# Attention scores from two half-height stacks: each head of a pair in its own half of the systolic array, and the two score products of a slot moved apart

## The reference, cut to what matters

```python
q, k = rope(q), rope(k)                           # (512, 32 heads, 16)
scores = einsum('bqhd,bkhd->bhqk', q, k) / sqrt(16)
scores = scores + (1.0 - causal) * MASK_VAL
probs = softmax(scores, axis=-1)
ctx = einsum('bhqk,bkhd->bqhd', probs, v)
y = (silu(h @ W_gate.T) * (h @ W_up.T)) @ W_down.T      # beside it, on the same rows
```

## Time and profile before

| | |
|---|---|
| median of 3 runs | 745.94 us (744.32 to 747.05) |
| the profiled execution | 744.25 us |
| its span, first to last instruction | 742.1 us |
| mean granted TensorE clock | 0.964 |
| PE busy | 653.9 us, 88% |
| DVE, POOL, ACT busy | 453.2, 403.7, 280.3 us |
| score stages, both batches | 167.2 and 166.1 us |

### The profile page before, as it was taken

The page is one execution under the profiler, slowest core; times in us unless marked ns, Lnnn a source line. Parts: engine busy times, 40 slices in busy tenths (PEclk is TensorE's granted clock), DMA queues, the critical chain, the costliest instruction groups (busy, mean ns, idle before and its releaser), DMA issues. The chain is left out here.

```text
span 742.1 us, 9827 instructions
## 1 busy us (share of the span) xinstructions
PE 653.9 (88%) x3229; PEld 468.4 (63%) x3229; DVE 453.2 (61%) x1086; ACT 280.3 (38%) x501; POOL 403.7 (54%) x593
## 2 busy tenths in 40 slices
PE   1967899999989998889999998989798979797993
PEld 1756566667756776666666765678676655555571
DVE  4977778756534493887785562459454434756347
ACT  2413445444543411344444455351222534142441
POOL 6476455545343556646554534439725778344465
PEclk9989999999999999999999999999998989999997
DMA  8287575753222226967575316534200000000003
GB/s 263 80 288 227 129 203 134 212 134 77 75 72 72 57 71 198 310 151 200 140 198 144 85 36 228 190 101 160 76 1 0 1 0 1 1 0 1 0 1 113
DMA packets 59731, 82.21 MB, mean 111 GB/s; under 512 B 18057, under 2 KB 26505, under 8 KB 59681
## 3 DMA queue, kind: packets, MB, share of 16 engines
q1 hardware_dynamic: 56016, 70.31, 33.4%
q10 hardware_dynamic: 3664, 11.28, 4.1%
HBM read 63.75 MB, written 26.47 MB: 122 GB/s over the span
## 5 line engine op out<-in xcount | busy, mean ns | idle before, releaser
L731 POOL TENSOR_TENSOR w_lo<-raw,w_hi 128x512 fp32r<-128x512 f32 x98 | 129.3, 1321 | 81.7 <-ACT w_hi L1251 76.8
L1294 ACT ACTIVATE probs_T<-score_ps 128x512 f32<-128x512 f32 x160 | 95.8, 599 | 156.2 <-PE score_ps L952 132.9
L1444 DVE CUSTOM_DVE_ANT_0 score_ps<-score_ps,causal 128x128 f32<-128x128 f32 (+2 forms) x256 | 103.0, 447 | 52.9 <-PE score_ps L938 28.6
L914 PE MATMUL proj_ps<-xn_hi,w_hi 128*128 128x512 f32 x240 | 100.9, 420 | 12.2 <-DVE by_sin L1520 7.5
L752 POOL TENSOR_SCALAR_AFFINE_SELECT probs_T<-probs_T 128x256 f32<-128x256 f32 (+1 forms) x160 | 56.5, 362 | 96.6 <-ACT probs_T L1294 96.6
L915 PE MATMUL proj_ps<-xn_hi,w_lo 128*128 128x512 f32 x240 | 96.7, 403 | 0.0
L916 PE MATMUL proj_ps<-xn_lo,w_hi 128*128 128x512 f32 x240 | 96.0, 400 | 0.0
L952 PE MATMUL score_ps<-q_st,kz 100*128 100x512 f32 (+3 forms) x256 | 65.4, 316 | 8.6 <-DVE row_max L1444 8.4
L952 PEld LDWEIGHTS score_ps<-q_st,kz 100*128 100x128 f32 x256 | 47.8, 188 | 26.0 <-DVE row_max L1444 15.1
L914 PEld LDWEIGHTS proj_ps<-xn_hi,w_hi 128*128 128x128 f32 x240 | 47.1, 196 | 22.7 <-issue 12.3
L916 PEld LDWEIGHTS proj_ps<-xn_lo,w_hi 128*128 128x128 f32 x240 | 46.7, 194 | 11.4
(11 more groups left out here) (288 smaller groups left out, 1496.0 us busy)
## 6 DMA issues: line engine op xcount, KB each, us to landing
raw<-w SPq DMA_DIRECT2D x98, 256.0 KB, 2.7
rows<-rows_hi SPq DMA_DIRECT2D x32, 256.0 KB, 3.6
arranged<-tern SPq DMA_DIRECT2D x96, 85.0 KB
q_st<-rows SPq DMA_DIRECT2D x16, 384.0 KB, 4.5
kz<-rows SPq DMA_DIRECT2D x32, 192.0 KB, 4.9
rows<-rows_lo SPq DMA_DIRECT2D x16, 256.0 KB, 4.1
gate_w<-arranged ACTq DMA_DIRECT2D x4, 704.0 KB, 6.9
up_w<-arranged ACTq DMA_DIRECT2D x4, 704.0 KB, 8.3
```

Source lines behind the costliest of these rows:

```text
L731: nc.gpsimd.tensor_tensor(w_lo[n % SPLIT][:, :], raw[n % RAW][:, :], F32(w_hi[n % SPLIT][:, :]), ALU.subtract).then_inc(unit_ready, 1)
L914: nc.tensor.matmul(acc, lh, rh, start=first, stop=False)
L1294: nc.scalar.activation(probs_T[gp % 3][:, 512 * i:512 * i + 512], score_bank(b, ("b", s - LAG))[:, :], ACT.Exp, scale=0.25).then_inc(probs ...
L1444: m = nc.vector.tensor_tensor_reduce(out=block, in0=block, in1=causal[:, S - w:], scale=1.0, scalar=-3e38, op0=ALU.add, op1=ALU.max, accum ...
```

## The change

Each head gets its own 50 contraction rows: 48 as before and 2 for its maximum (high and low part), head 0 of a pair on partitions 0 to 49, head 1 on partitions 64 to 113, in q_st and in k_st, which has no zeros. A matmul of a head then uses one half of the rows of the array, and the two heads' matmuls stand next to each other in the program. A pair has 3 A tasks and 3 B tasks, each with both heads, in two banks (score_ps for A, scoreT_ps for B; neither is doubled). A slot is now: A, half of the slot's triples, B, the other half. There are 48 + 5 = 53 score slots a batch, two triples in nearly every slot, and 8 triples ahead of slot 0. The two rows that meet the maximum are written to DRAM once (`edges`) and read with the rest; clearing kz and adding −1 on VectorE fall away. There is one bank for turns instead of two in this stage. The first Q and K unit of a batch use the score_ps banks; the second Q and K unit come after two feed-forward units instead of before; all three reads of a Q or K unit are made together. The down projection's operands are split one slot earlier.

```diff
+HEAD_ROWS = ROWS + 2
-LAG = 8
-SCORE_SLOTS = 5 * PAIRS + LAG
+A_TILES = [[(3, 0)], [(2, 0), (0, 384)], [(1, 0)]]
+B_TILES = [[(0, 0)], [(1, 0), (3, 384)], [(2, 0)]]
+WIDTH = (512, 512, 256)
+TASKS = 3 * PAIRS
+LAG = 5
+SCORE_SLOTS = TASKS + LAG
-Q_UNIT, K_UNIT, V_UNIT = (0, 6, 12, 18), (1, 7, 13, 19), 2
+Q_UNIT, K_UNIT, V_UNIT = (0, 8, 12, 18), (1, 9, 13, 19), 2
 def triple_slot(k):
-    return max(-1, (k - KC) * SCORE_SLOTS // (TRIPLES - KC))
+    return max(-1, (k - 2 * KC) * SCORE_SLOTS // (TRIPLES - 2 * KC))
...
+                for t, stack in enumerate((q_st, k_st)):
+                    for hh in range(2):
+                        sp.dma_start(F32(stack[n % 3][64 * hh:64 * hh + HEAD_ROWS, :, :]),
+                                     rows_d[b][t][c][h + hh:h + 4:2].rearrange("p r s -> r p s")).then_inc(stack_in[n % 3], 16)
...
-            for n in range(3):
-                nc.gpsimd.memset(F32(kz[n][:, :, :, :]), 0.0).then_inc(zeroed, 1)
...
+            def scores(b, j, x):
+                for part, (qt, c) in enumerate(A_TILES[x]):
+                    for hh in range(2):
+                        q, k = stacks(b, j, hh)
+                        m = nc.tensor.matmul(score_ps[:, hh, c:c + (qt + 1) * P], q[:, qt * P:(qt + 1) * P], k[:, 0:(qt + 1) * P],
+                                             start=part == 0, stop=True, skip_group_check=part > 0)
+                m.then_inc(score_done, 1)
+            def scores_T(b, j, x):
+                for part, (kt, c) in enumerate(B_TILES[x]):
+                    for hh in range(2):
+                        q, k = stacks(b, j, hh)
+                        m = nc.tensor.matmul(scoreT_ps[:, hh, c:c + S - kt * P], k[:, kt * P:(kt + 1) * P], q[:, kt * P:],
+                                             start=part == 0, stop=True, skip_group_check=part > 0)
+                m.then_inc(scoreT_done, 1)
...
                 for s in range(SLOTS):
                     if score_in(s):
-                        if bank_free(b, ("a", s)):
-                            pe.wait_ge(*bank_free(b, ("a", s)))
-                        score(score_bank(b, ("a", s)), b, j, i).then_inc(score_done, 1)
+                        if s:
+                            pe.wait_ge(part_ready, TASKS * b + s)
+                        scores(b, j, x)
+                    fill(b, s, 0)
+                    if prob_in(s):
+                        if x == 0:
+                            pe.wait_ge(*copied(b, ("max", j)))
+                        if s > LAG:
+                            pe.wait_ge(probs_ready, TASKS * b + s - LAG)
+                        scores_T(b, j, x)
                     if ctx_in(s) is not None:
                         turn(b, ("ctx", g), [ctx_sums[:, t * P:(t + 1) * P] for t in range(NT)])
-                    fill(b, s)
-                    if prob_in(s):
-                        score_T(score_bank(b, ("b", s - LAG)), b, j, i).then_inc(scoreT_done, 1)
+                    fill(b, s, 1)
...
             def max_out(b, j):
-                nc.scalar.activation(q_st[g % 3][2 * ROWS:2 * ROWS + 4, j % 2, :], turn_ps[n % 2][0:4, :], ACT.Copy)
+                for hh in range(2):
+                    m = nc.scalar.activation(q_st[g % 3][64 * hh:64 * hh + 2, j % 2, :], turn_bank(n)[32 * hh:32 * hh + 2, :], ACT.Copy)
...
-                        nc.scalar.activation(probs_T[gp % 3][:, 512 * i:512 * i + 512], score_bank(b, ("b", s - LAG))[:, :], ACT.Exp,
+                        nc.scalar.activation(probs_T[gp % 4][:, c:c + 2 * w].rearrange("p (h c) -> p h c", h=2), scoreT_ps[:, :, 0:w], ACT.Exp,
...
             def row_maxima(b, s):
+                for qt, c in A_TILES[x]:
+                    w = (qt + 1) * P
+                    for hh in range(2):
+                        block = score_ps[:, hh, c:c + w]
+                        m = nc.vector.tensor_tensor_reduce(out=block, in0=block, in1=causal[:, S - w:], scale=1.0, scalar=-3e38, op0=ALU.add,
+                                                           op1=ALU.max, accum_out=row_max[:, j % 2, 2 * qt + hh:2 * qt + hh + 1])
...
-            dve.wait_ge(zeroed, 3)
-            for n in range(3):
-                for hh in range(2):
-                    rows = kz[n][2 * ROWS:2 * ROWS + 4, :, hh, :]
-                    nc.vector.tensor_scalar(rows, F32(rows), extreme[2 * ROWS:2 * ROWS + 4, hh:hh + 1], None, ALU.add).then_inc(extreme_set, 1)
...
-                    if down_in(s + 1) is not None:
-                        f = down_in(s + 1)
+                    if down_in(s + 2) is not None:
+                        f = down_in(s + 2)
```

More of the change, by code:

```diff
@@ L101, in rest_in_slot, with written_in @@
 def rest_in_slot(s):
+    return [u for u in sorted(QK_OF) if u >= FILL and unit_slot(u) + 3 == s]
+def written_in(s):
     return [u for u in sorted(QK_OF) if u >= FILL and unit_slot(u) + 4 == s]
-def written_in(s):
-    return [u for u in sorted(QK_OF) if u >= FILL and unit_slot(u) + 5 == s]
 def read_in(s):
-    return next((g for g in range(1, GROUPS) if (1 if g == 1 else max(10 * g - 10, unit_slot(K_UNIT[g // 2]) + 9)) == s), None)
+    return next((g for g in range(1, GROUPS) if (1 if g == 1 else max(6 * g - 6, unit_slot(K_UNIT[g // 2]) + 7)) == s), None)
 def down_in(s):
@@ L119, in score_in @@
 def score_in(s):
-    return (s // 5, s % 5) if s < 5 * PAIRS else None
+    return divmod(s, 3) if s < TASKS else None
 def prob_in(s):
-    t = s - LAG
-    return (t // 5, t % 5) if 0 <= t < 5 * PAIRS else None
+    return divmod(s - LAG, 3) if 0 <= s - LAG < TASKS else None
 def max_in(s):
-    j = s // 5 - 1
-    return j if s % 5 == 1 and 0 <= j < PAIRS else None
+    j = s // 3 - 1
+    return j if s % 3 == 0 and 0 <= j < PAIRS else None
 def pv_in(s):
-    g, kt = divmod(s - 20, 10)
-    return (g, kt) if s >= 20 and g < GROUPS and kt <= NT else None
+    g, kt = divmod(s - 12, 6)
+    return (g, kt) if s >= 12 and g < GROUPS and kt <= NT else None
 def ctx_in(s):
[L139 to L146, removed]
-        if prob_in(s):
[L148 to L153, removed]
+    return (s - 17) // 6 if s >= 17 and (s - 17) % 6 == 0 and (s - 17) // 6 < GROUPS else None
 def turn_order():
@@ L174, with turn_banks @@
 TURNS = len(TURN)
-assert TURNS % 2 == 0
+def turn_banks():
+    banks = [kc % 2 for kc in range(KC)]
+    for b in range(B):
+        banks += [x % 2 if kind in ("xn", "ctxf") else 0 for kind, x in TURN]
+    banks += [2 * (kc % 2) for kc in range(KC)]
+    return [(k, banks[:n].count(k)) for n, k in enumerate(banks)]
+TURN_BANK = turn_banks()
 HI_BY_ACT = FILL
@@ L180, with copies_in @@
 RAW, SPLIT = 4, 5
-COPY_SLOTS = {0: range(14, 64), 1: range(14, 63)}
+COPIES = (50, 49)
+def copies_in(b, s):
+    at = [9 + 43 * n // COPIES[b] for n in range(COPIES[b])]
+    return at.count(s)
 W_GATE, W_UP, W_DOWN = range(3)
@@ L294, in program @@
     o_qk = at[0]
-    kz = [sb(f"kz{n}", [P, 2, 2, S], f32r) for n in range(3)]
+    k_st = [sb(f"k_st{n}", [P, 2, S], f32r) for n in range(3)]
+    o_pt0 = at[0]
+    at[0] += 10240
+    max_cols = sb("max_cols", [P, 2, NT, 34], f32r)
+    at[0] = o_qk + 24576
     o_x = at[0]
@@ L423, in program @@
     turned = sem("turned")
-    turn_free = [sem(f"turn_free{n}") for n in range(2)]
+    turn_free = [sem(f"turn_free{n}") for n in range(3)]
     xh_ready = sem("xh_ready")
@@ L947, in score_T, with stacks @@
[L947 to L954 removed]
+            def stacks(b, j, hh):
+                n = (GROUPS * b + j // 2) % 3
+                rows = slice(64 * hh, 64 * hh + HEAD_ROWS)
+                return q_st[n][rows, j % 2, :], k_st[n][rows, j % 2, :]
```

380 lines of the change are left out of this document (174 added, 206 removed).

## The result

The changed kernel takes **764.8 us** (median; 764.5 to 766.3), the kernel before 745.1 us beside it: a ratio of 1.026, 95% interval 1.023 to 1.029. Forecast were 736 us and a gain. The direction is wrong; the time is the one that rival 1 gave (764), just inside the range.

The account below looks back on a forecast made before the run. TensorE, busy 88% of the span, was taken to bound the kernel. Start -6.8, stages -2.4 and -1.3, and +0.5 ahead of batch 1's stage sum to -10.0 us: 745.9 becomes 736 us, range 715 to 766.

Parts of the forecast that it names:

- rival 1: Score stages: VectorE in order makes the next A wait, each stage keeps its 22 us; 764 us, chance 0.22.
- The price of a visit: Score stages: each visit to the half-height layout costs TensorE 0.40 us; 192 visits, 76.8 us, less 9.6 where they merge.
- Full overlap: Score matmuls: two heads in different row halves run at once, saving 36.8 us over both batches.
- Rivals 2 and 4: Score matmuls: 2, visits cost only 0.18 us, 694 us, chance 0.14; 4, fp32r halves don't overlap, 773 us, chance 0.06.
- The start: Ahead of the stages: without clears and VectorE's additions, slot 0 begins at 40.5 instead of 47.31 us, -6.8 us.
- rival 3: Rows' landing sets slot 0, only 1.3 of 6.8 us stays; group 2 waits 2.6 us with slow clock; 745 us, chance 0.16.
- What the new order removes: Score stages: maxima and exponentials fit the new slots of about 3.0 us; a stage after takes 164.8 us.
- What stays in a stage: Score stages: remaining stalls and slow clock sum to 8 us instead of 22.2 and 21.1.
- the sum of 145: Score stage of before: TensorE's priced work, 36.8 scores, 74.5 triples, 23.5 V product, 10 turns; the rest stalls and slow clock.
- the group-2 rows are asked for only two slots ahead: Score stages: read in slot 10 for slot 12, 6 us against some 2 of issues and 4.9 of landing; wait about 1.3.
- Both fit. VectorE, in order behind its maxima: Score slots: maxima and exponential are ready in time; VectorE has about 5.9 us of work a pair against TensorE's 9.3.
- At slot 0 ... about 2 us: Score stage's slot 0: two units finish at once, so the next triple waits for maxima and `ffn_out`, about 2 us.

Follow-up runs that it names:

- the run with 86 fewer: Changed kernel with a slot's two score products side by side (A, then B, then all of the slot's triples); 734.9 us, ratio 0.986 to before.
- clears put back: Changed kernel with six GpSimd clears and six small VectorE additions put back on the stacks, ahead of the first read of rows; 774.7 us.
- full-height kernel: Changed kernel with every score matmul contracted over all 128 rows, operands from the normalized input: no visits, no overlap of the heads; 755.5 us.
- short ropes: Kernel with group 2's rows read sooner (752.0 us), VectorE's four rope operations per score-stage Q or K unit cut to 8 of 512 columns; 748.6 us.
- context copy first: Changed kernel with ScalarE's copy of the context sums issued ahead of the slot's copy of a hidden unit; 761.1 us.
- units first: Changed kernel with VectorE finishing the two units done ahead of slot 0 before, not after, the maxima of slot 0; 762.0 us.
- rope split: Kernel with four edits at once (713.2 us), third read of a rope unit moved a slot later; 720.5 us.
- the kernel with the sooner read: Changed kernel with group 2's rows read in slot 9 instead of 10; 752.0 us.

## Why the prediction was wrong

- **The price of a visit** (0.40): right, 0.40 by the timeline and 0.37 by the run with 86 fewer. **Full overlap**: right, 39.6 us for 36.8. Rivals 2 and 4 are out. TensorE's own work in a stage after: 158.6 for 156.8, right. The Trainium skill, TensorEngine Tiling (Array Packing), says under Key Properties that a change of mode drains the engine: the trace agrees as far as it shows a delay at each change (0.32 us in place of 0.23 on entry), and the visits, 76.8 - 9.6 us by the price found, cost more than the 36.8 to 39.6 of the overlap.
- **The start**: right to 0.1 us, and for the stated cause (clears put back). Of rival 3 the first half is out; its second half, the full wait of group 2 with slow clock behind it, came, and larger than its 2.6 us.
- **The failed step** is "What the new order removes", with its "What stays in a stage ... Sum 8 us instead of 22.2 and 21.1". Both ends are off. Of the 22 us some 7 were TensorE's own: weight loads behind short matmuls, which the sum of 145 leaves out and no order of tasks removes (that they make up all 7 is argued from six slots of the full-height kernel). And 16 us of stalls and slow clock stayed in stage 0, 18 to 20 in stage 1, so the order removed nothing, while the change put 5 to 6.5 us of TensorE's own work into each stage (158.6 and 156 to 158 for 152). Its terms, in us:

| term | forecast | stage 0 | stage 1 |
|---|---|---|---|
| behind slot 0 | 2 | 2.1 | 2.1 |
| slow clock | 1.7 | 3.5 | 8.8 |
| rows of group 2 | 1.3 | 4.5 | 4.0 |
| ahead of the down projection | 1 | 3.2 | 3.2 |
| small gaps; waits for maxima | 2 | 3.1 | 1.7 |

- The **slow clock** is the largest miss of all over the two stages: 12.3 us where one short stretch in each, 3.4, was forecast. In the trace it stands at or behind waits (from 79.6 us in stage 0, where PE waits until 80.3; from 298.0, 311.7 and 335.6 in stage 1, where it waits until 298.7, 311.2 and 337.8). So the long waits that stayed cost more than their length; the shorter one of 1.7 us at 53.0 in stage 0 has no such stretch behind it.
- Within it, **"the group-2 rows are asked for only two slots ahead ..., about 1.3"** is the largest wait: 4.5 and 4.0 us, with slow clock 12.8 us for both batches by the run that mends it. The six microseconds were counted from the slot's start. Slot 10 began on TensorE at 70.65, but SyncE's queue reached the read only at 73.2, when the raw load ahead of it was released. The transfers then took what was forecast (7.1 us from the first issue to PE's start, for 2 + 4.9). So 2.5 us of the error are the queue, for which the forecast named no wait ahead of the read, and 0.9 the two slots, which gave 5.1 us of room instead of 6.
- **"Both fit. VectorE, in order behind its maxima"** was argued from the mean of a slot. Two such blocks in a row (columns of maxima, then a rope) don't fit, and 3.1 and 1.7 us of waits stay; short ropes remove them. This is rival 1's mechanism, at 4.8 us of waits in the whole run where its price was 28.
- **"At slot 0 ... about 2 us"**: right (2.1), though a part of it is ScalarE's. **"The last exponential ahead of the down projection, 1"**: 1.7 and 1.5 us, and the first is not the exponential but the copy of the context sums.
- **Behind the stages** only +0.5 us was forecast. The copy of the context sums costs 2.0 us in the down phase of each batch (context copy first). From the first down projection to the first output projection it is 43.2 us instead of before's 41.7 in batch 0, and 43.1 instead of 40.3 in batch 1, where before ran at full clock and after has a stretch at half clock behind the stage's last wait. From there to slot 0 of batch 1 it is 37.4 us instead of 35.4: the 2.8 us of extra triples were to fit into the wait of 3.4, but that shrank only to 2.6, since from the first issue of the read to PE's start it took 7.4 us instead of 5.5.
- Rival 1 gave 764 us for stalls that stay, and they stayed; but its price assumed 22 us a stage. The measured sum reaches the same number by 16 to 20 us in the stages, 5.8 behind them and block 1's 3.7. That the two agree to 1 us is luck.

Not settled: which executions get the longer half-clock stretches, and so how the some 8 us that the lower clock costs in every execution divide over the stages, the down phases and block 1; and why the full-height kernel waits 9.5 us for `row_max`, the changed one 4.8. Its slots are 0.15 us shorter, which would do it, but that was not tried.

## What to carry to other kernels

Count the changes of layout before the saving: here a slot's two products had to stand side by side for half-height matmuls to pay, and moving half of the triples turned 2.6% slower into 1.4% faster. "Span less priced work" is no measure of stalls that an edit can remove; add up the waits and the slow clock by name, and let the rest be work that isn't priced yet. Compare two kernels by span times granted clock too: it tells a gain in work from one in clock, and here one edit (units first) and one loss (rope split) were nearly clock alone. For each moved read or copy, find what stands ahead of it in its own queue and what that waits for: mean load per slot says nothing about it.

## What the runs showed of the hardware

- Matmuls of two row halves start 0 to 5 ns apart and share one stretch for fp32r too: 0.43 us with entry for two of 512 columns.
- A visit to 50-row matmuls among full-height ones of 512 columns costs 0.09 on entry, 0.20 on the visit itself (0.43 where 512 columns take 0.23; its weight load starts with it and not ahead of it) and 0.11 on the first matmul behind it: 0.40 us.
- A full-height 128-column matmul leaves the weight loads behind it exposed: the next pass took 0.28 to 0.29 us instead of 0.23, with no change of layout.
- One program differs by several us between executions through the granted clock: block 1 took 215.7 to 221.4 us in the profiles of this study, and 200 to 202 in each of them without the time lost at half clock (14.6 to 20.9 us). In the two whose windows are shown, 0.92 went with 217.7 us and 0.91 with 221.4.
- A long wait of TensorE can cost clock on top of its length: the kernel with the sooner read has 8 us less of waits for `k_st` (3.0 for 11.1) and is 4.9 us faster at full clock and 12.8 in all.
